# Loading eight samples in another order and over two DMA queues, in a four-stage convolution kernel

## Time and profile before

| what | value |
|---|---|
| median of 3 runs | 743.94 us |
| the profiled execution: its own time | 747.7 us |
| the profiled execution: its span | 745.9 us |
| PE busy | 604.6 us (81%) |
| DVE busy | 580.1 us (78%) |
| ACT busy | 554.8 us (74%) |
| POOL busy | 316.2 us (42%) |
| mean granted PE clock | 0.945 |

### The profile page before, as it was taken

The page is one execution under the profiler, slowest core; times in us unless marked ns, Lnnn a source line. Parts: engine busy times, 40 slices in busy tenths (PEclk is TensorE's granted clock), DMA queues, the critical chain, the costliest instruction groups (busy, mean ns, idle before and its releaser), DMA issues.

```text
span 745.9 us, 13366 instructions
## 1 busy us (share of the span) xinstructions
PE 604.6 (81%) x4142; PEld 165.7 (22%) x4142; DVE 580.1 (78%) x1006; ACT 554.8 (74%) x1057; POOL 316.2 (42%) x487
## 2 busy tenths in 40 slices
PE   0340763499999969999999999999999899899982
PEld 0210221122222212222222222222222222222220
DVE  1342576388898949988998899889988878799992
ACT  0212210189999949999999999999999999988882
POOL 2313015525791629526952794379204910630000
PEclk9985796799999979999999999999999999999996
DMA  5749569806785784665566556646650750083002
GB/s 102 136 77 179 116 145 200 158 8 144 142 193 102 163 167 100 143 153 114 111 138 144 114 124 140 146 102 142 140 116 1 164 119 0 12 197 74 1 1 56
DMA packets 72866, 85.53 MB, mean 115 GB/s; under 512 B 8674, under 2 KB 58354, under 8 KB 72818
## 3 DMA queue, kind: packets, MB, share of 16 engines
q1 hardware_dynamic: 68096, 78.58, 49.5%
q10 hardware_dynamic: 4722, 6.34, 4.7%
HBM read 9.14 MB, written 8.39 MB: 24 GB/s over the span
## 4 chain that ended last, share of the span: by engine, by line
PE 36%; DVE 24%; ACT 11%; DMA 9%; issue 8%; SPq 7%; POOL 2%; DVEq 1%; POOLq 0%
PE pz L788 17%; PE pc L734 8%; DMA xs<-in_x_dram 8%; DVE g L992 8%; PE pc L765 6%; ACT u L657 4%; DVE bn L935 4%; ACT u L660 3%; DVE u L989 3%; ACT u L663 3%; DVE g_last L992 3%; PE po L734 2%; SPq L347 2%; DVE box_sum L1008 2%; PE po L797 2%
## 5 line engine op out<-in xcount | busy, mean ns | idle before, releaser
L657 ACT ACTIVATE u<-pz 128x512 f32<-128x512 f32 x472 | 260.6, 601 | 74.1 <-PE pz L788 71.8
L992 DVE SCALAR_TENSOR_TENSOR g<-u,pz 128x512 f32<-128x512 f32 x384 | 247.7, 680 | 50.9 <-ACT u L660 46.6
L788 PE MATMUL pz<-g,wT 64*64 64x512 f32 x1536 | 271.9, 610 | 18.6 <-DVE g L992 16.7
L660 ACT ACTIVATE u<-u 128x512 f32<-128x512 f32 x472 | 275.8, 640 | 1.3
L765 PE MATMUL pc<-win,t 64*32 64x512 f32 x1392 | 101.7, 662 | 36.9 <-DMA win<-y 21.0
L788 PEld LDWEIGHTS pz<-g,wT 64*64 64x64 f32 x1536 | 68.8, 131 | 197.4 <-issue 195.9
L935 DVE BATCH_NORM_STATS2 bn<-xs 128x6 f32<-128x512 f32 (+1 forms) x128 | 84.3, 683 | 22.9 <-DMA xs<-in_x_dram 20.3
L992 DVE SCALAR_TENSOR_TENSOR g_last<-u,pz 128x512 f32<-128x512 f32 x128 | 82.6, 680 | 21.0 <-ACT u L660 19.3
L788 PE MATMUL pz<-stack,wT 64*64 64x512 f32 x512 | 87.6, 626 | 12.2 <-issue 6.4
L459 POOL TENSOR_TENSOR stat<-stat 128x1 f32<-128x1 f32 x32 | 6.2, 194 | 166.7 <-DVE stat L950 166.7
L734 PE MATMUL pc<-box_sum,box_mat 128*128 128x512 f32 x138 | 74.6, 635 | 1.2 <-DVE box_sum L1008 0.8
(11 more groups left out here) (96 smaller groups left out, 486.1 us busy)
## 6 DMA issues: line engine op xcount, KB each, us to landing
stack<-near_sum SPq DMA_DIRECT2D x90, 192.0 KB, 4.0
win<-y SPq DMA_DIRECT2D x56, 260.0 KB, 4.2
win<-y SPq DMA_DIRECT2D x56, 195.0 KB, 4.4
out_dram<-xs SPq DMA_DIRECT2D x8, 1024.0 KB
stack<-box_sum SPq DMA_DIRECT2D x60, 128.0 KB, 3.9
xs<-in_x_dram SPq DMA_DIRECT2D x7, 1024.0 KB
stack<-near_sum SPq DMA_DIRECT2D x30, 128.0 KB, 3.1
win<-y ACTq DMA_DIRECT2D x8, 260.0 KB, 9.2
```

The source lines that it names most:

```text
L657: act.activation(u[:, m, :], pz[:, m, :], ACT.Relu, scale=-1.0, bias=0.0).then_inc(relu_done, 1)
L660: act.activation(u[:, m, :], u[:, m, :], ACT.Exp, scale=-1.0).then_inc(exp_done, 1)
L788: last = pe.matmul(pz[to, m, :], wT[rows, l, rows], src, start=True, stop=True)
L992: dve.scalar_tensor_tensor(out=elus(l)[:, m, :], in0=u[:, m, :], scalar=-1.0, in1=pz[:, m, :], op0=ALU.add, op1=ALU.max).then_inc(g_writte ...
```

## The change

It touches SP's and ACT's lists of DMAs and the function `loaded`.

- Sample 0 is loaded as two DMAs, the even blocks of eight image rows by SP and the odd ones by ACT, as the first DMA of each.
- Sample 1 is loaded whole by SP, behind the h 0 windows of stage 0 for sample 0.
- The h 0 windows of stage 1 for sample 0 come ahead of the load of sample 2 on SP.
- Sample 4 is loaded by round 1, 5 by round 2, 6 by round 3 and 7 by round 4, each as the first thing in SP's list of the round.

Since sample 0 now counts 32 on `x_loaded`, `loaded(i)` has one formula.

```diff
         def loaded(i):
-            return LOAD if isinstance(i, int) and i == 0 else LOAD * (i + 2)
+            return LOAD * (i + 2)
...
+        xb = x.rearrange("b c (k two r) w -> b two r c k w", two=2, r=R)
+
+        def load_blocks(eng, i, odd):
+            half = xs[:, i * N:(i + 1) * N].rearrange("p (k two w) -> p two k w", two=2, w=W)
+            eng.dma_start(half[:, odd], xb[i, odd]).then_inc(x_loaded, 16)
...
             def load(i):
-                sp.dma_start(xs[:, bass.ds(i * N, N)].rearrange("p (k w) -> p k w", w=W), xv[i]).then_inc(x_loaded, 16)
-
-            def load_rows(i, first, end):
-                sp.dma_start(xs[first * C:end * C, i * N:(i + 1) * N].rearrange("p (k w) -> p k w", w=W),
-                             xv[i][first:end]).then_inc(x_loaded, 16)
-
-            load(0)
+                src = xv[i] if isinstance(i, int) else xv[bass.ds(i, 1)].rearrange("b r c k w -> (b r) c k w")
+                sp.dma_start(xs[:, bass.ds(i * N, N)].rearrange("p (k w) -> p k w", w=W), src).then_inc(x_loaded, 16)
+
+            load_blocks(sp, 0, 0)
             sp.dma_start(tables[0], con_early).then_inc(s_early, 16)
...
             def one(t):
+                if has(t + 3):
+                    sp.wait_ge(x_loaded, loaded(t + 2))
+                    sp.nop(nofuse=True)
+                    load(t + 3)
                 if has(t - 2):
                     store(t - 2)
...
-                first = isinstance(t, int) and t == 1
                 if has(t + 2):
...
-                if first:
-                    sp.wait_ge(x_loaded, loaded(4))
-                    load(5)
                 if has(t):
                     stacks(sp, t, 0)
                     stacks(sp, t, 1)
-                if first:
-                    sp.wait_ge(x_loaded, loaded(5))
-                    load(6)
-                    sp.wait_ge(x_loaded, loaded(6))
-                    load(7)
-
-            sp.wait_ge(x_loaded, LOAD)
+
+            sp.wait_ge(x_loaded, loaded(0))
             sp.dma_start(tables[2], con_late).then_inc(s_late, 16)
-            load_rows(1, 0, R // 2)
             sp.wait_ge(zeroed, N_ZEROED)
             windows0(sp, 0, (0,), True)
-            load_rows(1, R // 2, R)
-            sp.wait_ge(x_loaded, LOAD * 3)
+            load(1)
+            windows1(sp, 0, (0,), True)
+            sp.wait_ge(x_loaded, loaded(1))
             load(2)
-            windows1(sp, 0, (0,), True)
             sp.wait_ge(conv_mm[0], 2)
...
             stacks(sp, 0, 0)
-            sp.wait_ge(x_loaded, loaded(3))
-            load(4)
             rounds(sp, one)
...
         def _(act):
+            load_blocks(act, 0, 1)
             act.dma_start(tables[1], con_channel).then_inc(s_channel, 16)
```

## The result

The changed kernel takes 756.21 us (median of four runs, 754.49 to 756.32), beside 744.38 for the kernel before (743.35 to 747.26). The ratio is 1.0133, 95% interval 1.0098 to 1.0169: slower by 7 to 13 us. I had said 748.1, with a range up to 754. So the likeliest case had the right sign, and the size was wrong.

A forecast was written before the change was run, and what follows sets the result against it. Steady rounds were taken as full, the prologue as hanging on loads, round 2 as having a hole. +14.5 (parts 2 and 3 inside) and -10.3 gave +4.2 on the median 743.94: 748.1 us, range 740 to 754.

The forecast's parts named there:

- the likeliest case: Prologue: load 2 takes 19 to 22.5 us, giving a kernel time of 745 to 751 us; chance 0.50.
- part 4: Prologue, load 2 behind the windows of stage 1: takes 21.1 us, lands 14.5 us later, delays stage 1 of sample 0.
- The base of the sum: Profiled execution of before, 747.7 us, 3.8 above the median; the summed change was then added to the median, 743.94.
- Part 1: Rounds, loads of samples 4 to 7: hidden at the head of each round, closing round 2's hole, -10.3 us.
- the cover of some 4 us: Windows of stage 1 land before PE wants them, by 3.8 us in round 2 and 4.2 in round 3.
- Parts 2 and 3: Prologue: sample 0 in halves lands 1.7 us earlier; with sample 1 whole behind the windows, stage 0's convolution begins 2.7 earlier.
- Part 4's place: SP's queue in the prologue: load 2 goes out at 57.1 instead of 46.80, 10.3 us later.
- the prologue takes nothing back: Prologue behind stage 1 of sample 0: a chain of PE, DVE and windows that recovers none of the 14.5 us delay.
- Only because of written orders: Prologue: stage 1 of sample 0 depends on sample 2 only since DVE, PE and GpSimd have sample 2's work first.
- Rival 1: Prologue: load 2 not slowed by windows, 12.23 us, total 739.3; decides at a duration of 16.8 us; chance 0.12.
- Rival 2: Sample 0's load: both queues add up, each half takes 6.1 us, total 741.7; chance 0.08.
- Rival 3: Rounds 2 to 4: loads not hidden, windows 5 us later, total 750, or 758.4 if the hole's loss stays; chance 0.15.

The follow-up runs named there:

- the second pair: A second profiled execution of the kernel before and of the changed kernel, neither edited: 744.64 and 754.35 us.
- the two fastest kernels: Kernel before with loads 4 to 7 in the rounds and sample 0 in halves, 733.39 us; that with samples 0 to 2 as eight DMAs, sample 1 earlier, 730.30.

## Why the prediction was wrong

**The step that failed** is the term of part 4, "I take 21.1, the range 12.2 to 22.5". It measured 25.43, 25.51, and 23.82 with only this part changed, outside even the range. Two things were wrong in it. I named a second set of windows in the same paragraph ("and then ACT's windows of stage 0 for sample 1") and gave it no price; its price is 4.0 us, by the kernel that takes it off ACT's queue and puts it behind load 2 on SP's. And the row I took the 21.1 from, load 3 of the kernel before, is not a load that moves slowly beside windows. Its packets from 70.19 to 80.0, and from 80.0 to 91.3:

```profile
DMA packets 636, 1.79 MB, mean 183 GB/s; under 512 B 187, under 2 KB 206, under 8 KB 634
```

```profile
DMA packets 2157, 1.27 MB, mean 113 GB/s; under 512 B 63, under 2 KB 2104, under 8 KB 2156
```

In the first 10 us at most 19 pieces move: the load stands while both queues move windows. All the rest moves in 11 us, about as fast as a load alone. Load 2 in the changed kernel, from 57.57 to 62.0 and from 62.0 to 83.0, is another case:

```profile
DMA packets 280, 0.76 MB, mean 172 GB/s; under 512 B 95, under 2 KB 95, under 8 KB 280
```

```profile
DMA packets 2697, 2.86 MB, mean 136 GB/s; under 512 B 191, under 2 KB 2263, under 8 KB 2696
```

It stands for 4.4 us and then moves for 21, beside ACT's second set and beside SP's own next windows; behind load 3, SP issued nothing until 94.49. That the kernel without ACT's second set gave 21.45, so near to 21.1, is luck: there the load stood for some 5 us and moved for 16.5.

With 25.4 for 21.1 the sum becomes +8.5, 752.4 us on the median that was shown, which is within the interval of the ratio (+7.3 to +12.6).

**The base of the sum** was the smaller error. The profiled execution of before had a prologue 2.3 us longer than the second one of the same kernel. Taken from it, what the change adds up to round 1 is 17.0; from the second pair it is 19.6.

**Part 1 was right**: -10.3 foretold, -10.1 and -9.9 measured, and the cover of some 4 us in rounds 2 and 3 held. Alone the part wins 9 to 10 us.

**Parts 2 and 3 were right in sign and small.** Sample 0 lands 2.8 us earlier (1.7 foretold), the convolution of stage 0 begins at 34.59, 4.1 earlier (2.7 foretold). What they give back beside the rest can be estimated from the ratios, if the parts add: load 2 late loses 3.5%, the rounds win 1.3, the whole change loses 1.3, which leaves some 0.9% or 6 us for them, give or take 5 by the intervals. With load 2 in front they gave nothing in the one profile. The rule of the Trainium skill that I set beside part 2 (page "DMA: Bandwidth & Descriptors", section "Rules for kernel authors": two transfers to disjoint partition halves aren't worth it) is nearly borne out, although the halves here are alternate blocks of rows on all partitions: halves alone are worth 1.8 us, and the second queue 0.6 to 1.1 of sample 0's landing.

**Part 4's place was right**, in part by luck. Load 2 went out at 57.57 (57.1 foretold), from two errors that nearly cancel: the windows ahead of it went out at 50.30 and not 51.1, and SP took 7.3 us for them and not 6.0. Stage 1 began 12.3 us after it landed. That the prologue takes nothing back nearly held: of 19.4 us at stage 1, 17.0 reach round 1, and in the second pair 19.0 became 19.6.

**"Only because of written orders" was not the whole of it.** With those orders changed, the windows of stage 0 for sample 1, behind load 2 in SP's queue, hold PE next (12.68 us). I had looked at what waits for the load, and not at what is queued behind it.

**The rivals.** Rival 1 (load 2 not slowed) fell by 25.4 against its 16.8. Rival 2 (the queues add up) fell by the 11.39 us of sample 0, where it needed 6.1. Rival 3 (the loads in the rounds not hidden) fell by the 73.40 us of round 2.

**Open:** why sample 1 loaded whole makes windows land later when load 2 is in front (77.44 against 74.99), how much SP's own next windows cost load 2, and how much of the 3.1 us between the two fastest kernels is from the smaller DMAs.

## What to carry to other kernels

When a load moves within a queue, list what is queued behind it as well as what waits for it, and put it ahead of work whose followers stand in another engine's written order. Price each stream that will run beside it, one by one, and the ones ahead of it and behind it in its own queue too: a load that took 12.2 us alone took 16.9 with windows beside its second half, 21.5 with windows ahead of it, ACT's beside its first 6 us and SP's next ones beside its last 10, and 25.4 with a second set on ACT's queue as well. Before you carry the time of one transfer over to another, count its packets: the 21.1 us of load 3 were some 10 of standing and 11 of moving. Loads that aren't urgent can go one into each round where a cover of 4 us is left; that was worth 9 to 10 us here, and could be kept without the rest.

## What the runs showed of the hardware that was not expected

- Twice the DMA share (1.27 for 0.61) gave a load 119 GB/s instead of 104. The share adds up the times of packets, so it can pass 1, and in these rows it is no measure of what a load has left to win.
- Two loads issued right behind a set of windows in SP's queue, with another on ACT's, moved next to nothing at first: load 3 of the kernel before for 10 us, load 2 of the changed kernel for 4.4. Beside ACT's windows a load moved 0.37 MB in 6 us, without them 0.55.
- A DMA issue behind a whole load was held for 6.98 us, behind half a load for 1.14; five windows just behind load 2 took 15.43, and 14.60 and 17.73 in two other kernels, where such windows take some 5 with no load just ahead. With ACT's second set of windows gone they took 11.86. In these rows an issue was held for longer the longer the load ahead of it took, and everything behind it on that engine is late by it.
